# Seven block products in place of eight for queries and keys, with value blocks in four units

## The reference

```python
x1 = _ln(x) * (1.0 + scale1) + shift1
qkv = (x1 @ qkv_w + qkv_b).reshape(Bc, Tc, 3, H, DH)      # H = 16, DH = 128
q, k, v = (qkv[:, :, 0], qkv[:, :, 1], qkv[:, :, 2])
attn = jax.nn.softmax(jnp.einsum('bthd,bshd->bhts', q, k) * DH ** (-0.5), axis=-1)
attn_out = jnp.einsum('bhts,bshd->bthd', attn, v).reshape(Bc, Tc, INNER)
x = x + gate1 * (attn_out @ out_w + out_b)
```

## Time and profile before

| what | value |
|---|---|
| median of 3 runs | 359.79 us (358.42 to 359.95) |
| the profiled execution | 358.39 us |
| its span in the trace | 356.6 us |
| PE busy | 348.0 us, 98% of the span, 1998 matmuls |
| DVE, ACT, POOL busy | 59%, 56%, 30% |
| granted TensorE clock, mean | 0.997 |

### The profile page before, as it was taken

One profiled execution on the slowest core, in us unless ns is written; L12 is line 12 of the kernel. 1 busy time (PEld: TensorE's weight loads), 2 busy tenths in 40 slices (PEclk: granted clock), 3 DMA queues, 4 the chain that ended last, 5 costly groups with the idle time before them and its releaser, 6 DMA issues.

```text
span 356.6 us, 5788 instructions
## 1 busy us (share of the span) xinstructions
PE 348.0 (98%) x1998; PEld 300.7 (84%) x1998; DVE 210.0 (59%) x397; ACT 201.2 (56%) x524; POOL 107.5 (30%) x97
## 2 busy tenths in 40 slices
PE   8999899999999999999999999999999999999995
PEld 7788788888888888888888888888887888788875
DVE  5762347436535743643574354557875876677796
ACT  2675454545355454546555444656479645975593
POOL 2552222322733132272313237447451100000000
PEclk9999999999999999999999999999999999999998
DMA  5962031000303100030300003001000000000002
GB/s 177 367 202 85 4 118 61 0 0 2 119 0 118 59 0 0 0 118 3 115 0 0 0 0 118 2 0 61 1 2 0 1 2 0 2 0 0 3 29 88
DMA packets 12321, 16.52 MB, mean 46 GB/s; under 512 B 704, under 2 KB 8976, under 8 KB 12304
## 3 DMA queue, kind: packets, MB, share of 16 engines
q1 hardware_dynamic: 12160, 16.17, 13.5%
q10 hardware_dynamic: 144, 0.13, 0.1%
HBM read 15.25 MB, written 1.05 MB: 46 GB/s over the span
## 4 chain that ended last, share of the span: by engine, by line
PE 72%; issue 20%; DVE 4%; ACT 1%; DMA 1%; POOL 1%; POOLq 0%; ACTq 0%; DVEq 0%
PE bank L1010 17%; PE bank L1012 16%; PE bank L1011 16%; PE bank L1058 8%; PE bank L1039 8%; PE bank L1047 4%; DMA xt<-in_x_dram 1%; PE bank L1128 1%; DVE stats L670 1%; POOL rstd L344 1%; DVE hid_lo L736 1%; PE bank L1149 0%; DVE yT L762 0%; ACT o_hi L460 0%; DVE prob L690 0%
## 5 line engine op out<-in xcount | busy, mean ns | idle before, releaser
L349 POOL TENSOR_TENSOR prob<-prob,rinv 128x512 f32<-128x512 f32 x32 | 33.3, 1042 | 148.8 <-DVE rinv L826 148.8
L495 ACT ACTIVATE prob<-bank,nbias 128x128 f32<-128x128 f32 x128 | 45.3, 366 | 40.3 <-DVE nbias L814 40.3
L811 DVE TENSOR_REDUCE negmax<-bank 128x4 f32<-128x512 f32 x32 | 22.1, 690 | 74.1 <-PE bank L1039 74.1
L1010 PE MATMUL bank<-x_hi,wqk_hi 128*128 128x512 f32 x126 | 52.5, 417 | 0.0
L1012 PE MATMUL bank<-x_hi,wqk_lo 128*128 128x512 f32 x126 | 49.6, 394 | 0.0
L1011 PE MATMUL bank<-x_lo,wqk_hi 128*128 128x512 f32 x126 | 49.2, 390 | 0.0
L460 ACT ACTIVATE o_hi<-bank,bias 128x512 fp32r<-128x512 f32 x32 | 22.0, 688 | 38.3 <-PE bank L1058 38.3
L464 ACT ACTIVATE vals<-bank 128x512 f32<-128x512 f32 x32 | 19.0, 597 | 36.5 <-PE bank L1012 35.6
L1058 PEld LDWEIGHTS bank<-probT,vals 128*128 128x128 f32 x256 | 33.5, 191 | 2.5
L744 DVE TENSOR_SCALAR kT<-bank,bias 128x512 f32<-128x512 f32 x32 | 24.0, 751 | 19.2 <-PE bank L1012 19.1
L1039 PE MATMUL bank<-kT,qT 128*128 128x128 f32 x256 | 33.9, 275 | 1.0 <-DVE ada L852 1.0
(11 more groups left out here) (174 smaller groups left out, 768.8 us busy)
## 6 DMA issues: line engine op xcount, KB each, us to landing
raw_qk<-in_L_cond_qkv_w_dram SPq DMA_DIRECT2D x6, 512.0 KB, 4.5
raw_v<-in_L_cond_qkv_w_dram SPq DMA_DIRECT2D x4, 512.0 KB, 4.1
raw_o<-in_L_cond_out_w_dram SPq DMA_DIRECT2D x4, 512.0 KB, 3.5
xt<-in_x_dram SPq DMA_DIRECT2D x2, 512.0 KB, 4.4
xr<-in_L_cond_ada_w_dram SPq DMA_DIRECT2D x1, 1024.0 KB, 8.6
raw_w<-in_L_cond_ffn_w_dram SPq DMA_DIRECT2D x2, 512.0 KB, 6.8
t_raw<-in_L_ffn_W_fc_dram SPq DMA_DIRECT2D x4, 256.0 KB, 3.7
t_raw<-in_L_ffn_W_proj_dram SPq DMA_DIRECT2D x4, 256.0 KB, 3.9
```

Source lines behind the costliest of these rows:

```text
L349: nc.gpsimd.tensor_tensor(e, e, rinv[:, j % 2, :].unsqueeze(2).broadcast_to([P, SQ, P]), ALU.mult).then_inc(norm_done, 1)
L495: e = nc.scalar.activation(prob[:, j % 2, s, :], bank[BS][:, s * P:(s + 1) * P], ACT.Exp, bias=nbias[:, j % 2, s:s + 1], scale=SCALE, accu ...
L811: nc.vector.tensor_reduce(negmax[:, j % 2, :], bank[BS][:, :].rearrange("p (s t) -> p s t", s=SQ), axis=AX.X, op=ALU.max, negate=True).the ...
L1010: nc.tensor.matmul(dst, ah, bh, start=start and n == 0, stop=False)
```

## The change

For 13 of the 16 heads (all but heads 0 and 1 of the first group and head 3 of the last) the queries and keys of both quads are made together. The weights of a head (query and key, each of 2 feature blocks) and the activations (2 feature blocks, each of 2 quads) are 2x2 block matrices, and their product is made of seven block products (`pair_p1` to `pair_p7`, 3 matmuls each) in place of eight, with sums of weight blocks (`ws`) and of activation blocks (`xc`) as operands. The sums are made once: `x_sums` on DVE in the lead-in (4 subtractions or additions of 512 columns, then high and low parts of 2048 columns), `weight_sums` on POOL per group (4 of 512 columns), with `ws_hi_part` on ACT and `ws_lo_part` on POOL per head.

The pair of a head is made in one **pair unit** (units 0, 1, 2 and 4; unit 4 makes head 0 of the next group). Four of the products accumulate on the same bank BQ, and ACT copies intermediate states out of it (`copy_p1`, `copy_u2`, `copy_u3`) before PE may go on in it; DVE adds such a copy to another bank's product for queries and keys (`pair_q0`, `pair_k1`, `pair_q1`), ACT makes the last (`pair_k0`). Quad 1's queries and keys are kept in `q1T` and `k1T` until units 4 to 7. Value blocks stand in units 3 (four of them), 5 (two), 6 and 7 (one each). The output product of a pair unit is cut in two halves that stand between products.

The high and low parts of the next group's query and key weights are made in units 3, 5, 7 and 0, those of the value weights in unit 4, all behind `keep_v` and `o_hi` on ACT. The sums lie in the memory of `w1_lo` and `w2_lo`. The core of the diff:

```diff
-        V_AT = {1: (4, 5), 2: (6, 7), 5: (0, 1), 6: (2, 3)}
+        BE = BO + 1
+        PAIR_AT = {4: 0, 0: 1, 1: 2, 2: 3}
+        V_AT = {3: ((4, BQ), (5, BK), (6, BE), (7, BQ)), 5: ((0, BQ), (1, BK)), 6: ((2, BQ),), 7: ((3, BK),)}
+        V_LAST = {3: ((4, BQ), (5, BK)), 4: ((6, BE),), 5: ((7, BE),)}
+        WQK_AT = {3: 0, 5: 1, 7: 2, 0: 3}
...
+        def pair_head(G, j):
+            return (G + 1, 0) if j == 4 else (G, PAIR_AT[j])
...
+            def weight_sums(G, a0=0):
+                n = 4 * G
+                s = slice(a0 * P, HG * P)
+                raw = ws
+                pool.wait_ge(wqk_in, 32 * G + 32)
+                nc.gpsimd.tensor_tensor(raw[:, 0, s], raw_qk[:, 2, s], raw_qk[:, 3, s], ALU.add).then_inc(ws_raw, 1)
+                nc.gpsimd.tensor_tensor(raw[:, 2, s], raw_qk[:, 0, s], raw_qk[:, 2, s], ALU.subtract).then_inc(ws_raw, 1)
+                pool.wait_ge(ws_raw, n + 1)
+                nc.gpsimd.tensor_tensor(raw[:, 1, s], raw[:, 0, s], raw_qk[:, 0, s], ALU.subtract).then_inc(ws_raw, 1)
+                pool.wait_ge(ws_raw, n + 3)
+                nc.gpsimd.tensor_tensor(raw[:, 3, s], raw_qk[:, 1, s], raw[:, 1, s], ALU.subtract).then_inc(ws_raw, 1)
+            def ws_lo_part(G, a):
+                s = slice(a * P, (a + 1) * P)
+                lo_part(ws_lo[:, :, s], ws[:, :, s], ws_hi[:, :, s], ws_h, pair(G, a), ws_l)
...
+                    pool.wait_ge(p3_mm, pair(G, 3))
+                    weight_sums(G + 1)
                 normalise(UG * G + j, j)
                 if j == 0:
                     wqk_lo_part(3, HG * G + 4)
...
                 if j == 1:
+                    if isinstance(G, int):
+                        ws_lo_part(0, 2)
+                        ws_lo_part(0, 3)
                     wo_lo_part(0, 2 * G + 1)
                 if j == 2:
                     wo_lo_part(1, 2 * G + 2)
...
-                if j == 3:
+                if j == 4:
                     for k in range(KD):
                         wv_lo_part(k, KD * G + KD + k + 1)
-                if j == 5:
-                    wqk_lo_part(0, HG * G + HG + 1)
-                    wqk_lo_part(1, HG * G + HG + 2)
-                if j == 6:
-                    wqk_lo_part(2, HG * G + HG + 3)
+                if j in (3, 5, 7):
+                    wqk_lo_part(WQK_AT[j], HG * G + HG + WQK_AT[j] + 1)
+                    ws_lo_part(G + 1, WQK_AT[j])
...
+            def copy_p1(G, a):
+                act.wait_ge(p1_mm, pair(G, a))
+                act.nop(nofuse=True)
+                nc.scalar.activation(p1, bank[BQ][:, :], ACT.Copy).then_inc(p1_cp, 1)
...
-            def unit(G, j, vs, more, last=False):
+            def unit(G, j, last=False):
                 i = UG * G + j
+                pair_unit = j in PAIR_AT and not last
                 if last and j >= UG - 2:
                     keep_p(i - 1)
+                if pair_unit:
+                    copy_p1(*pair_head(G, j))
                 act.wait_ge(nb_done, i + 1)
-                for s in range(SQ):
-                    e = nc.scalar.activation(prob[:, j % 2, s, :], bank[BS][:, s * P:(s + 1) * P], ACT.Exp,
-                                             bias=nbias[:, j % 2, s:s + 1], scale=SCALE,
-                                             accum_out=rowsum[:, j % 2, s:s + 1])
-                e.then_inc(exp_done, 1)
-                if more:
-                    G1, j1 = (G, j + 1) if j < UG - 1 else (G + 1, 0)
-                    keep_q(G1, j1)
+                exps(i, j, range(2))
+                if pair_unit:
+                    copy_u2(*pair_head(G, j))
+                exps(i, j, range(2, SQ))
+                if pair_unit:
+                    copy_u3(*pair_head(G, j))
...
                     wo_hi_part(1, 16 * G + 16)
+                if pair_unit:
+                    pair_k0(*pair_head(G, j))
+                vs = (V_LAST if last else V_AT).get(j, ())
+                for n, (b, src) in enumerate(vs):
+                    if n == len(vs) // 2 and not (last and len(vs) == 1):
+                        o_hi_part(*before(G, j))
+                    keep_v(b, v_count(G, b), src)
+                if not vs or (last and len(vs) == 1):
+                    o_hi_part(*before(G, j))
+                if j == 0:
+                    ws_hi_part(G, 3)
                 if not last:
                     if j == 2:
                         act.wait_ge(tern_in, 32 * G + 32)
                         nc.scalar.activation(t_bf[:, :], t_raw[:, :, :].rearrange("p a b -> p (a b)"), ACT.Copy).then_inc(t_cast, 1)
-                    if j == 3:
+                    if j == 4:
                         for k in range(KD):
                             wkeep_v(k, 16 * G + 32)
-                    if j == 5:
-                        wqk_hi_part(0, 32 * G + 64)
-                        wqk_hi_part(1, 32 * G + 64)
-                    if j == 6:
-                        wqk_hi_part(2, 32 * G + 64)
+                    if j in (3, 5, 7):
+                        wqk_hi_part(WQK_AT[j], 32 * G + 64)
+                        ws_hi_part(G + 1, WQK_AT[j])
...
+            for n in range(2):
+                act.wait_ge(xc_raw, 4)
+                hi_part(xc_hi[:, 2 * n:2 * n + 2, :], xc[:, 2 * n:2 * n + 2, :], xc_h)
+            ws_hi_part(0, 2)
+            ws_hi_part(0, 3)
+            o_hi_part(0, 0)
+            wo_hi_part(0, 16)
+            copy_p1(0, 2)
+            copy_u2(0, 2)
+            copy_u3(0, 2)
+            pair_k0(0, 2)
...
+            def pair_q0(G, a):
+                dve.wait_ge(p1_cp, pair(G, a))
+                dve.wait_ge(p2_mm, pair(G, a))
+                joined(qT[:, :], bank[BK][:, :], HG * G + QB + a, p1, q0_done)
+            def pair_k1(G, a):
+                dve.wait_ge(u3_cp, pair(G, a))
+                dve.wait_ge(p5_mm, pair(G, a))
+                joined(k1T[:, a, :], bank[BE][:, :], HG * G + KB + a, u3[:, :], k1_done)
...
+            def x_sums():
+                raw = xc
+                nc.vector.tensor_tensor(raw[:, 0, :], xfull[:, 0, :], xq0[:, 0, :], ALU.subtract).then_inc(xc_raw, 1)
+                nc.vector.tensor_tensor(raw[:, 2, :], xfull[:, 1, :], xfull[:, 0, :], ALU.subtract).then_inc(xc_raw, 1)
+                dve.wait_ge(xc_raw, 1)
+                nc.vector.tensor_tensor(raw[:, 1, :], xfull[:, 1, :], raw[:, 0, :], ALU.subtract).then_inc(xc_raw, 1)
+                dve.wait_ge(xc_raw, 3)
+                nc.vector.tensor_tensor(raw[:, 3, :], xq0[:, 1, :], raw[:, 1, :], ALU.subtract).then_inc(xc_raw, 1)
...
+            def x_sums_lo():
+                for n in range(2):
+                    c = slice(2 * n, 2 * n + 2)
+                    dve.wait_ge(xc_h, n + 1)
+                    nc.vector.tensor_tensor(xc_lo[:, c, :], xc[:, c, :], xc_hi[:, c, :].bitcast(F32),
+                                            ALU.subtract).then_inc(xc_l, 1)
             def o_lo_part(G, j):
...
-                    keep_k(G1, j1)
+                if pair_unit:
+                    pair_k1(*pair_head(G, j))
+                if first:
...
-            unit(0, 1, V_AT[1], True)
+            x_sums()
+            unit(0, 1)
+            keep_qk1(0, 0, 3, BQ, BK)
+            keep_qk1(1, 0, 4, BE, BY)
+            x_sums_lo()
+            pair_q0(0, 2)
+            pair_k1(0, 2)
...
+            def pair_p1(G, a):
+                pe.wait_ge(wqk_l, head(G, a) + 1)
+                pe.wait_ge(q1_done, head(G, a))
+                pe.wait_ge(k1_done, head(G, a))
+                product(BQ, "raw", 0, a, "raw", (0, 0), start=True).then_inc(p1_mm, 1)
+            def pair_p2(G, a):
+                product(BK, "raw", 1, a, "raw", (1, 0), start=True).then_inc(p2_mm, 1)
+            def pair_p6(G, a):
+                pe.wait_ge(ws_l, pair(G, a))
+                pe.wait_ge(p1_cp, pair(G, a))
+                product(BQ, "sum", 1, a, "sum", 1).then_inc(p6_mm, 1)
+            def pair_p5(G, a):
+                product(BE, "sum", 0, a, "sum", 0, start=True).then_inc(p5_mm, 1)
+            def pair_p7(G, a):
+                pe.wait_ge(u2_cp, pair(G, a))
+                product(BQ, "sum", 2, a, "sum", 2).then_inc(p7_mm, 1)
+            def pair_p4(G, a):
+                pe.wait_ge(u3_cp, pair(G, a))
+                product(BQ, "raw", 3, a, "sum", 3).then_inc(p4_mm, 1)
+            def pair_p3(G, a):
+                pe.wait_ge(k1_done, head(G, a) + 1)
+                product(BE, "sum", 3, a, "raw", (1, 1)).then_inc(p3_mm, 1)
...
+            def pair_unit(G, j):
+                i, (g, a) = UG * G + j, pair_head(G, j)
+                scores(G, j)
+                if j == 4:
+                    pe.wait_ge(v_done, v_count(G, 7))
+                if j == 0:
+                    pe.wait_ge(v_done, v_count(G - 1, 3))
+                pair_p1(g, a)
+                transpose_p(i - 1, (j - 1) % 2)
+                pair_p2(g, a)
+                pair_p6(g, a)
+                pair_p5(g, a)
+                out_half(*before(G, j, 2), 0)
```

(36 more changed lines are left out.)

315 lines of the change are left out of this document (200 added, 115 removed).

## The result

| what | before | after |
|---|---|---|
| median of the runs beside each other | 359.11 us (358.38 to 359.95) | 392.59 us (391.15 to 393.5) |
| the profiled execution, its span | 358.39, 356.6 us | 392.42, 390.6 us |
| PE busy, matmuls | 348.0 us, 98%, 1998 | 355.8 us, 91%, 1959 |
| granted TensorE clock, mean | 0.997 | 0.98 |

The change makes the kernel slower: ratio 1.092, 95% interval 1.088 to 1.096. The forecast was 380.5 with a range to 387; slower was right, the size was not.

The account below looks back on a forecast made before the run. PE's instruction stream, busy 98% of the span, was taken as the time. Eight waits, (a) to (h), of 30.8 us less 9.0 for 39 matmuls gave +21.8 on 358.39, 380.2, forecast as 380.5; range 366 to 387.

Parts of the forecast that it names:

- (a): Unit 4: `pair_p1` waits for head 0's query and key weights, behind value block 7's copy: 1.9 three times, +5.8 us.
- (b): Unit 5: first value block waits for value weights, whose high parts stand behind `o_hi`: 2.3 three times, +7.0 us.
- (c): Unit 0: PE waits ahead of `pair_p1` for value block 3's copy, behind `o_hi` on ACT: 0.7 three times, +2.1 us.
- (d): Twelve pair units: `pair_p4` waits for `copy_u3` of the accumulating bank: 0.3 each, +3.6 us.
- (e): `pair_q1` in units 1 and 2: the next unit's `pair_p1` waits for it, 0.27 six times, +1.6 us.
- (f): Units 3 and 6: DVE's `nbias` waits for POOL's running instruction, so `o_lo` delays PE's output product: +5.1 us.
- (g): Last group: next weights' high parts behind `o_hi` and a value copy make POOL's `normalise` late for unit 5's transposes: +2.5 us.
- (h): Lead-in: `pair_p1` waits 3.8 for DVE's low parts of the activation sums; net of the old 1.0 wait, +3.1 us.
- through the waits of a loop pass in order: The prediction's method: added engine work judged by where it stands, taking a loop pass's waits one after another.
- the clock falls: Rival: PE's new long idle waits lower the granted clock; one fall in the lead-in 382, at all seven 392; chance 0.08.
- Milder: Rival: (a), (b), (c) and (h) hold but (d) to (f) mostly don't appear: 370 to 375 us; chance 0.22.
- faster: Rival: ACT and POOL have weights ready, nothing of (a), (b), (h): 357 us, or 353 with half the rest; chance 0.10.

Follow-up runs that it names:

- wqk_early: Changed kernel with ACT making the next group's head 0 query and key high part right behind unit 3's exponentials, outside the last group: 390.68 us, ratio 1.087.
- kept_busy: Changed kernel with identity transposes keeping PE at work in three kinds of long waits (unit 4, unit 5, lead-in): 389.77 us, ratio 1.083.
- last_order: Changed kernel with ACT, in the last group, making ternary cast and next weights' high parts ahead of value copies and `o_hi`: 386.3 us, ratio 1.077.

## Why the prediction was wrong

By its own steps, from the distances of PE's starts:

| step | forecast | measured |
|---|---|---|
| 39 matmuls | -9.0 | 1959 in the trace: -9.0 |
| (a) | 5.8 | 1.88, 1.89, 1.88: 5.7 |
| (b) | 7.0 | 2.25, 2.23, 2.23: 6.7 |
| (c) | 2.1 | 0.80 three times: 2.4 |
| (d) | 3.6 | 0.34 twelve times: 4.1 |
| (e) | 1.6 | 0.24 five times, 0.10 once: 1.3 |
| (f) | 5.1 | 0.89 and 0.77, three times each: 5.0 |
| (g) | 2.5 | 2.4 |
| (h) | 3.1 | 4.33 less the 1.0, and 0.4 at the first keys: 3.7 |
| the cast in the last group | nothing | 2.8 |
| first 512-column matmul behind a wait | nothing | 1.5 |
| the clock, four falls | a rival | 6.2 |

The eight terms were forecast at 30.8 us and came to 31.3, and each was released by the instruction that was named. So the mechanism was right, step by step; "through the waits of a loop pass in order" held, and (f), read off a single 0.41 beside a median of 0.17, came out to a tenth. With (c) at 0.80 for 0.7 and (d) at 0.34 for 0.3, the errors are of that size throughout. In (h) two errors partly cancelled: DVE alone needs 2.35 and not 2.6, and POOL's turn added 1.07. The Trainium skill's rule (SBUF — State Buffer, "Who interferes with whom"), which the forecast left out, gave 4.4; the two outcomes seen, 3.7 here and 5.45 - 1.0 + 0.4 = 4.9 in wqk_early, lie on both sides of it.

Two steps failed. The first is "the clock falls". It was held at a chance of 0.08, with one fall (382) or seven (392) as its two cases, and argued from the 1.0 us idle in the earlier trace rows, which the clock survives, while the new waits are two to four times as long. Four falls came, at 1.5 to 1.6 us each, as forecast for one (1.6). Without their 6.2 us the time would be 386.4, inside the range. The rival should have been part of the forecast, as a chance for each long wait; the middle, three or four falls, would have given 386.

The second is the search of the last group, which looked for POOL's lateness alone: (g) followed the high parts that moved behind `o_hi` through to `normalise`, and left out the cast that moved with them, and DVE, which waits for it with the maximum and `o_lo` behind. That is 2.8 us; without it alone the time would be 389.8, still outside the range.

A smaller term was put at nothing without a reason: the first matmul behind a wait takes 0.34 to the next one. (d) has that in its measured 0.34; for (a), (b), (c), (f), the lead-in and the cast it comes on top, an estimate of 1.5 us from the distances at these places (0.11 each at (a), (f), the lead-in and the cast, less at (b) and (c)). In the profiled execution, -9.0 + 31.3 + 2.8 + 1.5 + 6.2 = 32.8 of the 34.0 us are laid at a place; 1.2 stay open.

The forecast's own arithmetic has two slips that decided nothing. It names the median's 1.4 us above the profiled execution and then adds only 0.3 of it (380.2 to 380.5), and its lower bounds add up to 371.2 and not 370, its upper ones to 384.6 and not 386.

"Milder" was wrong because (d) to (f) all came; "faster" because none of (a), (b), (h) was covered, at 56% and 30% load.

## What to carry to other kernels

A fused step that needs its operands earlier is to be judged by what stands ahead of the operands' producers on their engines, not by those engines' load: here the place of instructions and waits, and one small operation on another engine, made +9.2% into -1.4% with no matmul changed. When PE's waits get as long as 2 us, price each with a possible fall of the clock, of about 1.6 us, in the forecast itself. And follow every instruction of a moved block, small ones too.

## What the runs showed of the hardware

- Behind four waits of 2.2 to 4.2 us the granted clock was 1.2 GHz for some eight matmuls of 512 columns, from 0.8 us after PE had resumed (40.61) or from its first matmul on (218.02, 0.50 to the next). Of three equal waits (82.08, 150.05, 218.02) only the last brought it, and which do so changed from kernel to kernel. One fall costs 1.5 to 1.6 us. Transposes of the identity in the wait of the lead-in held the clock up (0.88 to 1.00). The Trainium skill, TensorE: Matmul & The Clock Gate, "HAM oscillation", ties the slow level to idle gaps: kept_busy and last_order agree.
- Behind a wait the first 512-column matmul mostly takes 0.34 to the next, in place of 0.23; straight behind 128-column ones, without a wait, 0.31. So a wait of 0.23 in a stream of 512-column matmuls costs 0.34.
- DVE and GpSimd, each subtracting one SBUF operand from another, took turns by whole instructions, with two outcomes for the same code: 3.42 or 4.53 us on DVE, 5.8 or 4.7 on POOL, and 2.35 and 3.8 where they are alone.
- The kernel before, whose longest wait inside the attention is 1.0 us, also ran in two groups, 358.3 to 358.7 us at a mean clock of 0.996 or 0.997 and 359.8 to 360.2 at 0.991 to 0.995. The difference of about 1.5 is what one fall costs; the slower group has no trace here, so where the clock was low in it is not shown.
